# Building one quarter of the scan's transposed input with a diagonal matrix on TensorE, and alternating ScalarE's two kinds of work

## The chip, the cores and the metric

One core of a Trainium2 chip runs the whole program. The metric is the device time of one execution in microseconds (us), as the median of several runs. The engines of the core are called PE (TensorE; PEld are its weight loads), ACT (ScalarE), DVE (VectorE), POOL (GpSimd) and SP (SyncE, which issues DMAs here).

## What is computed

Two layers. Layer 0 is a bidirectional selective state-space block (forward and backward over time) followed by a gated MLP; layer 1 is attention and another MLP. The change touches only the state-space scan. Cut to it:

```python
B, L, D_MODEL, COND = (2, 512, 256, 256)     # the inputs in fact have L = 1024
D_STATE, EXPAND = (64, 2)                     # D_INNER = 512
...
xs = jax.nn.silu(xs)
proj = xs @ xproj_w
dt = jax.nn.softplus(proj[..., :D_INNER] + dt_bias)
Bm = proj[..., D_INNER:D_INNER + D_STATE]
Cm = proj[..., D_INNER + D_STATE:]
A = -jnp.exp(A_log)

def step(hst, ins):
    dt_t, B_t, C_t, x_t = ins
    dA = jnp.exp(dt_t[:, :, None] * A)
    hst = hst * dA + (dt_t * x_t)[:, :, None] * B_t[:, None, :]
    y_t = jnp.einsum('bds,bs->bd', hst, C_t)
    return (hst, y_t)
...
h_fwd = _ssm(h, ...fwd weights...)
h_bwd = jnp.flip(_ssm(jnp.flip(h, 1), ...bwd weights...), 1)
```

For each of the 64 states, the recurrence runs along time for each of 512 channels: the decay is `exp(dt * a)`, the input is `dt * x * B`, and the output sums state times `C` over the states.

## The kernel before, in words

**Units and states.** The scan is cut into 8 units (`UNITS`), each one direction, one batch element and one half (512 steps, `HALF`) of the sequence. A unit has 64 states (`DS`), so the main loop runs over 512 pairs `w = 64 * u + st`. The channels lie in 4 blocks `f` of 128 (`NI`), the 512 time steps in 4 blocks `c` of 128 (`TB`). In half of the units (0, 2, 4 and 6) the scan starts from zero and its last column is saved (`carry`); in units 1, 3, 5 and 7 it starts from that.

**One state, engine by engine.** ACT makes the scan's input with time on the partitions, `uT[t, channel] = dtxT[t, channel] * b[t]`: 4 activations of 128x512 with a scale of one value per partition (line L868), into one of two buffers (`w % 2`). It also makes the decays, 4 exponentials of 128x512 (L875), into one of two buffers. PE turns `uT` over: for each channel block `f`, 4 transposes of 128x128 (`turn_u`, L1421) into one of 3 PSUM banks. DVE runs one scan of 128x512 for each `f` (L1119), reading a decay and a PSUM bank and writing the state's values `hs` (a ring of 3 states). POOL multiplies the values by the row of `C` in two products of 128x1024 (L647), and in units 0, 2, 4 and 6 first copies the last columns to `carry` (L643, with a wait for that copy). PE turns each product back and adds it up over the states in 4 PSUM banks, 16 more transposes for a state (`turn_h`, L1426; for the first state of a unit `first_state` also adds 16 plain f32 products of 128x128, L1446).

**Who waits for whom.** ACT's `uT(w)` waits until PE has turned all of state `w - 2` (`u_full`); its decay `(w, f)` waits for the scan `(w - 2, f)`. `turn_u` waits for all 4 pieces of `uT(w)` and for the scan three tiles back (the bank). A scan waits for its decay, its bank and, in the ring, for the reduction of state `w - 3`. All queues are in order. PE's is `turn_u(w, f)`, then `reduce_state(w - 2, f)`, and after each odd `f` one piece of other work.

**Other work between the states.** The projections of the next unit and the output of the unit before are cut into pieces that PE runs inside the loop (`pe_turn`, `place_turns`): an f32 product of 128x512 at L1213 is a piece, two pieces go into a state, a tile of two products takes one state of two, and a tile of four products (`dt`, `bc`, `out`) two states of three. There are 44 such pieces in a unit (8 for `xs`, 8 for `zs`, 16 for `dt`, 4 for `bc`, 8 for `out`). ACT copies their results (L740, L712, L753, L766) after its 8 activations of a state, and has two bursts in a unit: at state 31 the SiLU of `xs` and `zs` (L745, L747), at state 46 the softplus (L724, L733, L735), both with reloads of its function table. At state 48 POOL has one more product of 128x2048 (L628).

The loop on ACT, and the turn on PE:

```python
if w >= 2:
    act.wait_ge(s["u_full"], NI * (w - 1))
for c in range(TB):
    act.activation(uT[:, w % 2, c], dtxT[:, u % 2, c], ACT.Copy, scale=bT[:, u % 2, c, st:st + 1])\
       .then_inc(s["uT_ready"], 1)
```

Of the kernel before, what the change touches and what calls it, by code (L numbers as in the profile page):

```python
# [11 lines left out]
P = 128  # L12
B, L, DM = 2, 1024, 256
DI, DS = 512, 64
# [4 lines left out]
NI = DI // P  # L19
# [18 lines left out]
SCAN_TILES = UNITS * DS  # L38
# [5 lines left out]
SUMS_STEP = 4  # L44
U_TILES = SCAN_TILES * NI
U_BANKS = 3
RING = 3
PIECES = {"out": 4, "bc": 4, "dt": 4, "down": 4}
SILU_STEP, SOFTPLUS_STEP, DTX_STEP = 31, 46, 48
# [3 lines left out]
def build(nc, t):  # L53
    F32, I32, BF16 = mybir.dt.float32, mybir.dt.int32, mybir.dt.bfloat16
    ALU, ACT, AX = mybir.AluOpType, mybir.ActivationFunctionType, mybir.AxisListType

    ctx = ExitStack()
    with ctx:
        def sb(name, shape, dt=F32):
            return ctx.enter_context(nc.sbuf_tensor(name, shape, dt))  # L60

        def sem(name):
            return ctx.enter_context(nc.semaphore(name))
# [4 lines left out]
        def cut(at, *dims):  # L68
            n = 1
            for d in dims:  # L70
                n *= d
            v = arena[:, at:at + n]
            if len(dims) == 2:
                v = v.rearrange("p (a b) -> p a b", b=dims[1])
            if len(dims) == 3:
                v = v.rearrange("p (a b c) -> p a b c", b=dims[1], c=dims[2])
            if len(dims) == 4:
                v = v.rearrange("p (a b c d) -> p a b c d", b=dims[1], c=dims[2], d=dims[3])
            return v
# [12 lines left out]
        xs = cut(R_XS, 2, NI, HALF)  # L92
        dt_ = cut(R_DT, 2, NI, HALF)
        zsT = cut(R_ZS, 2, HALF // P, DI)

        TB = HALF // P
        dtxT = cut(R_DTX, 2, TB, DI)
        uT = cut(R_UT, 2, TB, DI)  # L100
        decay = cut(R_DA, 2, NI, HALF)
        hs = cut(R_UH, RING, NI, HALF)
        c_rows = cut(R_C, 2, 2, HALF)
# [40 lines left out]
        bT = sb("bT", [P, 2, TB, DS])  # L144
        skip_w = sb("skip_w", [P, 2, NI, P])
        attn_sb = skip_w.rearrange("p a b c -> p a (b c)")
        ident = sb("ident", [P, P])
# [41 lines left out]
        s = {n: sem(n) for n in names}  # L189
# [7 lines left out]
        eaters, first = [], {}  # L197
# [69 lines left out]
        def pe_turn(u, st):  # L267
            return TURN[u].get(st)


        def act_turns(u, st):

            step, long_ = TURN[u].get(st - 1), TURN[u].get(st - 2)
            todo = [long_] if long_ and PIECES.get(long_[0]) else []
            todo += [step] if step and not PIECES.get(step[0]) else []
            if step and step[0] == "sum":
                todo.append(("std",) + step[1:])
            back = TURN[u].get(st - 4)
            if back and back[0] == "mean":
                todo.append(("square",) + back[1:])  # L280
            if u == UNITS - 1:
                return todo
            if st == SILU_STEP:
                todo.append(("silu", u + 1))
            if st == SOFTPLUS_STEP:
                todo.append(("softplus", u + 1))
            return todo
# [90 lines left out]
        place_tiles(START, lambda g: 4 + g % 4)  # L378
        u_before = [holder.get(4 + n) for n in range(U_BANKS)]
        for u in range(UNITS):  # L380
            for st in range(DS):
                if pe_turn(u, st):
                    place_tiles([pe_turn(u, st)], lambda g: 4 + U_BANKS)
        for n in range(U_TILES - U_BANKS, U_TILES):
            holder[4 + n % U_BANKS] = ("u", n)
        place_tiles(LATE, lambda g: 4 + g % 4)
        place_tiles(END, lambda g: 4 + g % 4)

        def eaten(g, who):

            return sum(e == who for e in eaters[:g + 1])
# [20 lines left out]
        def take_u(pe, n):  # L412

            free_bank(pe, u_before[n] if n < U_BANKS else ("u", n - U_BANKS))
            return psum[:, 4 + n % U_BANKS, :]

# [30 lines left out]
        for v in range(BLOCKS):  # L447
            for m in range(BLOCK):
# [4 lines left out]
                if rows_at(v, m):  # L453
                    half, u, j = rows_at(v, m)
# [151 lines left out]
        def _(pool):  # L606
# [23 lines left out]
            for u in range(UNITS):  # L630
                d, b, hi, half = unit(u)
                for st in range(DS):
                    w = u * DS + st
                    p = w // 2
                    h_now = hs[:, w % RING]
                    if w % 2 == 0:
# [38 lines left out]
        def _(act):  # L675
# [99 lines left out]
            def do(order):  # L775

                for kind, *at in order:
                    if kind == "square":
                        square(*at)
                    if kind == "std":  # L780
                        std(*at)
                    if kind in ("xs", "zs"):
                        u, f = at
                        (silu_path if kind == "xs" and u == 0 else raw_path)((xs if kind == "xs" else zsT)[:, u % 2, f], first[kind, u, f])
                    if kind == "silu":
                        silu(*at)
                    if kind == "dt":
                        raw_dt(*at)
                    if kind == "softplus":
                        log_dt(*at)  # L790
                    if kind == "bT":
                        copy_bT(*at)
                    if kind == "dtxT":
                        copy_dtxT(*at)
                    if kind == "yT":
                        copy_yT(*at)
                    if kind == "decay rate":
                        act.wait_ge(s["ssm_small_in"], 80)
                        act.activation(a_neg[:, :, :, :], a_neg[:, :, :, :], ACT.Exp).then_inc(s["a_exp"], 1)
                        skip_weights()  # L800
                    if kind == "up":
                        silu_up(*at)
                    if kind == "qk":
                        copy_qk(*at)
                    if kind == "v":
                        copy_v(*at)
                    if kind == "any key":
                        softmax_scale()
                    if kind == "first part":
                        first_part(*at)  # L810
                    if kind == "second part":
                        act.wait_ge(s["rest_ready"], at[0] + 1)
                        act.activation(qk_parts[:, 1], qk, ACT.Copy).then_inc(s["mid_ready"], 1)
# [42 lines left out]

            do(START)
            act.wait_ge(s["a_ready"], 1)
            for u in range(UNITS):
                d, b, hi, half = unit(u)  # L860
                for st in range(DS):
                    w = u * DS + st
                    if st == 0:
                        act.wait_ge(s["tile_free_act"], eaten(first["dtxT", u, TB - 1], "a"))
                    if w >= 2:
                        act.wait_ge(s["u_full"], NI * (w - 1))
                    for c in range(TB):
                        act.activation(uT[:, w % 2, c], dtxT[:, u % 2, c], ACT.Copy, scale=bT[:, u % 2, c, st:st + 1])\  # L868
                           .then_inc(s["uT_ready"], 1)
                    if st == 0:  # L870
                        act.wait_ge(s["dt_ready"], NI + u)
                    for f in range(NI):
                        if w >= 2:
                            act.wait_ge(s["scan_done"], NI * (w - 2) + f + 1)
                        act.activation(decay[:, w % 2, f], dt_[:, u % 2, f], ACT.Exp, scale=a_neg[:, d, f, st:st + 1])\  # L875
                           .then_inc(s["decay_ready"], 1)
                    do(act_turns(u, st))

            do(LATE)
# [20 lines left out]
            for v in range(BLOCKS):  # L900
                for m in range(BLOCK):
                    w = v * BLOCK + m
# [19 lines left out]
        def _(dve):  # L922
# [183 lines left out]
            for u in range(UNITS):  # L1106
                d, b, hi, half = unit(u)
                for st in range(DS):
# [3 lines left out]
                    for f in range(NI):  # L1112
                        n = NI * w + f
                        if w >= RING:
                            dve.wait_ge(s["reduce_done"], NI * (w - RING) + f + 1)
                        dve.wait_ge(s["decay_ready"], n + 1)
                        dve.wait_ge(s["u_full"], n + 1)
                        way = slice(None, None, -1) if d else slice(None)
                        dve.tensor_tensor_scan(hs[:, w % RING, f, way], decay[:, w % 2, f, way],  # L1119
                                               psum[:, 4 + n % U_BANKS, way],  # L1120
# [88 lines left out]
        def _(pe):  # L1209
# [204 lines left out]
            def turn_u(w, f):  # L1414

                n = NI * w + f
                if f == 0:
                    pe.wait_ge(s["uT_ready"], TB * (w + 1))
                dst = take_u(pe, n)
                for c in range(TB):  # L1420
                    o = pe.transpose(dst[:, c * P:(c + 1) * P], uT[:, w % 2, c, f * P:(f + 1) * P], ident[:, :])  # L1421
                o.then_inc(s["u_full"], 1)

            def turn_h(w, f, c):

                return pe.matmul(psum[:, c, f * P:(f + 1) * P], hs[:, w % RING, f, c * P:(c + 1) * P], ident[:, :],  # L1426
                                 is_transpose=True, start=False, stop=w % DS == DS - 1 and f == NI - 1)
# [28 lines left out]
            for w in range(SCAN_TILES + 2):  # L1456
                u, st = divmod(w, DS)
# [132 lines left out]
```

## Time and profile before

| | |
|---|---|
| median of 3 runs | 3658.23 us (3657.68 to 3658.84) |
| the profiled execution's own time | 3660.08 us |
| its span, from the first to the last instruction | 3658.3 us |
| mean granted TensorE clock | 0.965 |
| the scan (first scan to the end of the last) | 64.8 to 2832.4 us, 76% of the span |
| busy: PE, PEld, DVE, ACT, POOL | 86%, 63%, 82%, 87%, 70% |

The times are read from one profiled execution. PE's busy time is no measure of its capacity, since matmuls overlap; the distance between the starts of two is. The scan takes three quarters of the span, so each engine's share is read inside it, by unit.

### The profile page before, as it was taken

The numbers are of one execution on the slowest core, as the hardware profiler recorded it, in microseconds if no ns is written. First come the engines' busy times: TensorE is split into PE (matmuls) and PEld (weight loads), VectorE is DVE, ScalarE is ACT, GpSimd is POOL, SyncE is SP. The second block draws the span as 40 slices with busy tenths as digits, with TensorE's granted clock in tenths as the row PEclk, the third lists the DMA queues.
The fourth block names the chain that finished last, engine by engine and source line by source line (L and its number), as shares of the span: only waits on it lengthen the run. The fifth ranks groups of instructions, "written<-read, shape, count | busy, mean of one in ns | idle before, by whom it ended". The sixth has DMA issues, their size and how long they took to land.

```text
span 3658.3 us, 55690 instructions
## 1 busy us (share of the span) xinstructions
PE 3164.3 (86%) x20898; PEld 2320.4 (63%) x20898; DVE 3009.3 (82%) x2916; ACT 3179.8 (87%) x5112; POOL 2568.8 (70%) x1577
## 2 busy tenths in 40 slices
PE   8888888889878888988888889878888898999999
PEld 5777777777767777777777777767677432222244
DVE  4888998899889989988998899889999478888241
ACT  6999999999999999999999999999999236777621
POOL 2889998899999979999998899999789000000000
PEclk8999999999999999999999999999999998999999
DMA  2111111111112111111111111112111043121000
GB/s 100 51 44 47 53 53 49 47 53 53 53 42 78 53 48 53 47 54 47 57 54 49 47 53 53 52 44 70 47 47 47 12 104 70 25 29 18 1 6 17
DMA packets 65197, 175.91 MB, mean 48 GB/s; under 512 B 13697, under 2 KB 17537, under 8 KB 64673
## 3 DMA queue, kind: packets, MB, share of 16 engines
q1 hardware_dynamic: 64930, 172.36, 15.3%
q8 instruction: 166, 2.72, 0.3%
q14 instruction: 101, 0.83, 0.1%
HBM read 162.83 MB, written 9.44 MB: 47 GB/s over the span
## 4 chain that ended last, share of the span: by engine, by line
ACT 59%; PE 23%; POOL 11%; DVE 4%; issue 1%; DMA 0%; SPq 0%; DVEq 0%; POOLq 0%; ACTq 0%
ACT arena L868 27%; ACT arena L875 26%; PE psum L1213 10%; POOL arena L647 10%; PE psum L1513 3%; PE psum L1502 3%; PE psum L1477 2%; PE psum L1421 2%; DVE row_max L1166 2%; PE psum L1426 2%; POOL arena L628 1%; DVE arena L1119 1%; PE psum L1446 1%; POOL carry L643 1%; ACT arena L740 1%
## 5 line engine op out<-in xcount | busy, mean ns | idle before, releaser
L647 POOL TENSOR_TENSOR arena<-arena 128x1024 f32<-128x1024 f32 x1024 | 2425.2, 2382 | 172.4 <-DVE arena L1119 128.8
L1421 PE MATMUL psum<-ident,arena 128*128 128x128 f32 x8192 | 1278.7, 280 | 326.0 <-ACT arena L868 268.3
L1421 PEld LDWEIGHTS psum<-ident,arena 128*128 128x128 f32 x8192 | 974.8, 143 | 608.6 <-ACT arena L868 377.0
L868 ACT ACTIVATE arena<-arena,bT 128x512 f32<-128x512 f32 x2048 | 1309.9, 719 | 28.0 <-PE psum L1421 27.8
L1426 PE MATMUL psum<-ident,arena 128*128 128x128 f32 x8192 | 1262.8, 278 | 78.2 <-POOL arena L647 77.3
L1119 DVE TENSOR_TENSOR_SCAN arena<-arena,psum 128x512 f32<-128x512 f32 x1024 | 1179.9, 1204 | 175.2 <-PE psum L1421 94.3
L875 ACT ACTIVATE arena<-arena,a_neg 128x512 f32<-128x512 f32 x2048 | 1311.2, 720 | 1.7 <-DVE arena L1119 1.4
L1119 DVE TENSOR_TENSOR_SCAN arena<-arena,carry,psum 128x512 f32<-128x512 f32 x1024 | 1225.5, 1260 | 96.3 <-ACT arena L875 58.3
L1426 PEld LDWEIGHTS psum<-ident,arena 128*128 128x128 f32 x8192 | 973.5, 143 | 115.5 <-POOL arena L647 115.5
L1213 PE MATMUL psum<-arena 128*128 128x512 f32 x1472 | 709.1, 604 | 12.2 <-issue 5.0
L1213 PEld LDWEIGHTS psum<-arena 128*128 128x128 f32 x1472 | 258.7, 195 | 202.9 <-issue 193.8
L1166 DVE TENSOR_REDUCE row_max<-psum 128x1 f32<-128x512 f32 x512 | 317.9, 676 | 58.1 <-PE psum L1477 56.7
L908 ACT ACTIVATE arena<-psum 128x512 f32<-128x512 f32 x512 | 273.6, 599 | 81.8 <-PE psum L1502 80.1
L670 POOL TENSOR_TENSOR arena<-skip_w 128x512 f32<-128x512 f32 x16 | 20.3, 1267 | 403.6 <-DVE skip_w L1192 403.6
L643 POOL COPY carry<-arena 128x2 f32<-128x2 f32 x512 | 103.9, 203 | 126.4 <-DVE arena L1119 126.0
L1477 PE MATMUL psum<-arena 97*128 97x512 bf16 x512 | 161.3, 393 | 20.1 <-DVE row_max L1166 17.1
L1502 PE MATMUL psum<-arena 100*128 100x512 bf16 x512 | 160.6, 387 | 4.5 <-ACT arena L908 3.4
L663 POOL MEMSET arena<- 4x4096 f32 x3 | 10.7, 3579 | 185.9 <-DVE arena L1041 106.2
L1513 PE MATMUL psum<-arena 128*32 128x512 f32 x1024 | 136.4, 604 | 4.6 <-ACT skip_w L885 4.5
L1502 PEld LDWEIGHTS psum<-arena 100*128 100x128 bf16 x512 | 35.8, 97 | 158.5 <-ACT arena L908 125.0
L825 ACT ACTIVATE arena<-psum,b_up 128x512 f32<-128x512 f32 x32 | 22.0, 687 | 113.4 <-PE psum L1213 113.4
L1477 PEld LDWEIGHTS psum<-arena 97*128 97x128 bf16 x512 | 50.7, 99 | 99.7 <-DVE row_max L1166 45.8
(115 smaller groups left out, 1070.9 us busy)
## 6 DMA issues: line engine op xcount, KB each, us to landing
arena<-bc_dram SPq DMA_DIRECT2D x256, 512.0 KB, 3.7
arena<-qk_dram SPq DMA_DIRECT2D x96, 128.0 KB
qk_dram<-arena SPq DMA_DIRECT2D x12, 512.0 KB, 4.9
arena<-in_x SPq DMA_DIRECT2D x4, 512.0 KB, 10.7
arena<-in_up_w SPq DMA_DIRECT2D x1, 2048.0 KB, 12.0
out_xT<-arena SPq DMA_DIRECT2D x8, 256.0 KB, 2.2
arena<-in_mlp_w SPq DMA_DIRECT2D x3, 512.0 KB, 6.5
arena<-in_fwd_xproj_w SPq DMA_DIRECT2D x1, 1280.0 KB, 9.8
```

Source lines behind the costliest of these rows:

```text
L647: pool.tensor_tensor(h_now[:, f:f + NI // 2], h_now[:, f:f + NI // 2], c_row, ALU.mult)\
L868: act.activation(uT[:, w % 2, c], dtxT[:, u % 2, c], ACT.Copy, scale=bT[:, u % 2, c, st:st + 1])\
L875: act.activation(decay[:, w % 2, f], dt_[:, u % 2, f], ACT.Exp, scale=a_neg[:, d, f, st:st + 1])\
L908: act.activation(probs[:, w % 4, jj], psum[:, n % 3, :], ACT.Exp)\
L1119: dve.tensor_tensor_scan(hs[:, w % RING, f, way], decay[:, w % 2, f, way], psum[:, 4 + n % U_BANKS, way], carry[:, st, f:f + 1] if hi else ...
L1166: dve.tensor_reduce(row_max[:, qt, j, kh:kh + 1], side_bank("scores", w), axis=AX.X, op=ALU.max)\
L1213: o = pe.matmul(dst, lhsT, rhs, start=k == 0, stop=k == len(pairs) - 1)
L1421: o = pe.transpose(dst[:, c * P:(c + 1) * P], uT[:, w % 2, c, f * P:(f + 1) * P], ident[:, :])
L1426: return pe.matmul(psum[:, c, f * P:(f + 1) * P], hs[:, w % RING, f, c * P:(c + 1) * P], ident[:, :], is_transpose=True, start=False, stop ...
L1477: pe.matmul(take_side(pe, "scores", w), stack[u % STACKS][0:PLAIN, 0, j, qt * P:(qt + 1) * P], stack[u % STACKS][0:PLAIN, 1, j, tok(kh)], ...
L1502: pe.matmul(psum[:, n % 3, :], stack[u % STACKS][0:ROWS, 1, j, kt * P:(kt + 1) * P], stack[u % STACKS][0:ROWS, 0, j, tok(qh)], start=True, ...
L1513: o = pe.matmul(psum[32 * j:32 * j + 32, 4, :], v_aug[:, b, kt, hg, 32 * j:32 * j + 32], probs[:, 2 * (kt % 2) + j // 2, j % 2], start=kt ...
```

## The change

Of the 4 time blocks `c` of the scan input, the first (`DIAGS = 1`) is no longer made by ACT over 512 channels. ACT writes only a 128x128 diagonal matrix, the identity times `b[t]`, into `uT[:, w % 2, 0, 0:128]`; PE then multiplies `dtxT` (as weights) by this diagonal, a plain f32 matmul of 128x128, which turns and scales at once. The other three blocks stay transposes.

The order on ACT changes as well: the 4 pieces for `uT(0)` come ahead of the loop, and in state `w` each exponential `f` is followed by piece `f` of `uT(w + 1)`. So `uT` of a state is made one state earlier, and the wait of `uT(w + 1)` for `u_full` stands behind the first exponential of state `w`: it asks for all turns up to state `w - 1`. It is asked for before each piece.

```diff
+DIAGS = 1
...
             do(START)
             act.wait_ge(s["a_ready"], 1)
+            def scan_input(w, c):
+
+                u, st = divmod(w, DS)
+                if st == 0 and c == 0:
+                    act.wait_ge(s["tile_free_act"], eaten(first["dtxT", u, TB - 1], "a"))
+                if w >= 2:
+                    act.wait_ge(s["u_full"], NI * (w - 1))
+                src = ident[:, :] if c < DIAGS else dtxT[:, u % 2, c]
+                act.activation(uT[:, w % 2, c, 0:P if c < DIAGS else DI], src, ACT.Copy,
+                               scale=bT[:, u % 2, c, st:st + 1]).then_inc(s["uT_ready"], 1)
+
+            for c in range(TB):
+                scan_input(0, c)
             for u in range(UNITS):
                 d, b, hi, half = unit(u)
                 for st in range(DS):
                     w = u * DS + st
-                    if st == 0:
-                        act.wait_ge(s["tile_free_act"], eaten(first["dtxT", u, TB - 1], "a"))
-                    if w >= 2:
-                        act.wait_ge(s["u_full"], NI * (w - 1))
-                    for c in range(TB):
-                        act.activation(uT[:, w % 2, c], dtxT[:, u % 2, c], ACT.Copy, scale=bT[:, u % 2, c, st:st + 1])\
-                           .then_inc(s["uT_ready"], 1)
                     if st == 0:
                         act.wait_ge(s["dt_ready"], NI + u)
                     for f in range(NI):
...
                         act.activation(decay[:, w % 2, f], dt_[:, u % 2, f], ACT.Exp, scale=a_neg[:, d, f, st:st + 1])\
                            .then_inc(s["decay_ready"], 1)
+                        if w + 1 < SCAN_TILES:
+                            scan_input(w + 1, f)
                     do(act_turns(u, st))
...
                 for c in range(TB):
-                    o = pe.transpose(dst[:, c * P:(c + 1) * P], uT[:, w % 2, c, f * P:(f + 1) * P], ident[:, :])
+                    if c < DIAGS:
+                        o = pe.matmul(dst[:, c * P:(c + 1) * P], dtxT[:, w // DS % 2, c, f * P:(f + 1) * P],
+                                      uT[:, w % 2, c, 0:P], start=True, stop=True)
+                    else:
+                        o = pe.transpose(dst[:, c * P:(c + 1) * P], uT[:, w % 2, c, f * P:(f + 1) * P], ident[:, :])
                 o.then_inc(s["u_full"], 1)
```

## Rows read from the trace of the kernel before

**Rows 1.** The page: busy time of the engines, and the chain that ended last.

```profile
PE 3164.3 (86%) x20898; PEld 2320.4 (63%) x20898; DVE 3009.3 (82%) x2916; ACT 3179.8 (87%) x5112; POOL 2568.8 (70%) x1577
...
ACT 59%; PE 23%; POOL 11%; DVE 4%; issue 1%; DMA 0%; SPq 0%; DVEq 0%; POOLq 0%; ACTq 0%
ACT arena L868 27%; ACT arena L875 26%; PE psum L1213 10%; POOL arena L647 10%; PE psum L1513 3%; PE psum L1502 3%; PE psum L1477 2%; PE psum L1421 2%; DVE row_max L1166 2%; PE psum L1426 2%; POOL arena L628 1%; DVE arena L1119 1%; PE psum L1446 1%; POOL carry L643 1%; ACT arena L740 1%
```

**Rows 2.** Windows, one for each unit: busy time and count by engine.

```profile
core 0: us, PE busy (x) PEld busy (x) DVE busy (x) ACT busy (x) POOL busy (x), PEclk, DMA share, GB/s
64.80:425.60 360.80, 296.87 (x2172) 254.27 (x2170) 309.43 (x270) 351.41 (x554) 319.62 (x251) 0.95 0.13 46
...
768.40:1112.00 343.60, 291.94 (x2203) 250.63 (x2201) 301.08 (x264) 341.49 (x547) 322.14 (x253) 0.97 0.17 57
1112.00:1454.50 342.50, 291.22 (x2208) 251.60 (x2209) 312.35 (x266) 337.08 (x539) 312.13 (x135) 0.97 0.15 51
...
2484.30:2832.40 348.10, 294.23 (x2196) 254.69 (x2196) 330.95 (x287) 336.81 (x531) 306.43 (x134) 0.96 0.15 48
```

**Rows 3.** Timeline of ACT over one state of unit 2: start, length, instructions.

```profile
1101.36 2.56 ACT L868 ACTIVATE arena<-arena,bT 128x512 f32<-128x512 f32 x4
1103.81 2.56 ACT L875 ACTIVATE arena<-arena,a_neg 128x512 f32<-128x512 f32 x4
1106.27 1.33 ACT L868 ACTIVATE arena<-arena,bT 128x512 f32<-128x512 f32 x2
```

**Rows 4.** Waits in units 1 to 6: us in total, times, longest us.

```profile
ACT arena L868 <- PE psum L1421: 18.3, 12, 4.0
...
POOL arena L647 <- DVE arena L1119: 88.3, 134, 8.6
```

**Rows 5.** Timeline of POOL late in unit 2.

```profile
1086.55 2.38 POOL L647 TENSOR_TENSOR arena<-arena 128x1024 f32<-128x1024 f32 x1
1088.86 0.19 POOL L643 COPY carry<-arena 128x2 f32<-128x2 f32 x1
1089.13 2.38 POOL L647 TENSOR_TENSOR arena<-arena 128x1024 f32<-128x1024 f32 x1
```

**Rows 6.** Timeline of unit 3: DVE, and POOL, each with nothing to wait for.

```profile
1141.68 16.48 DVE L1119 TENSOR_TENSOR_SCAN arena<-arena,carry,psum 128x512 f32<-128x512 f32 x14
...
1398.92 18.68 POOL L647 TENSOR_TENSOR arena<-arena 128x1024 f32<-128x1024 f32 x8
```

**Rows 7.** Timeline of ACT before the scan: the one scaled identity.

```profile
32.51 2.43 ACT L772 ACTIVATE skip_w<-ident,d_skip 128x128 f32<-128x128 f32 x8
```

**Rows 8.** Timeline of PE in unit 1: transposes and plain f32 products of 128x128.

```profile
438.34 2.05 PE L1446 MATMUL psum<-skip_w,arena 128*128 128x128 f32 x8 [0.53 <-POOL arena L647]
...
442.96 0.60 PE L1421 MATMUL psum<-ident,arena 128*128 128x128 f32 x4
443.40 1.06 PE L1446 MATMUL psum<-skip_w,arena 128*128 128x128 f32 x8
444.29 0.60 PE L1426 MATMUL psum<-ident,arena 128*128 128x128 f32 x4
```

**Rows 9.** Timeline of PE in unit 2: a piece, and what follows it.

```profile
1008.03 1.02 PE L1213 MATMUL psum<-arena 128*128 128x512 f32 x2
1008.89 0.60 PE L1421 MATMUL psum<-ident,arena 128*128 128x128 f32 x4
```

**Rows 10.** Groups by line and shape, whole span: busy, mean ns, idle before.

```profile
L628 POOL TENSOR_TENSOR arena<-arena 128x2048 f32<-128x2048 f32 x7 | 31.8, 4541 | 0.0
L875 ACT ACT_TABLE_LOAD x24 | 30.8, 1283 | 0.4
```

**Rows 11.** Timeline of ACT in unit 2, around its burst at state 46.

```profile
1008.05 2.56 ACT L875 ACTIVATE arena<-arena,a_neg 128x512 f32<-128x512 f32 x4
...
1018.21 2.54 ACT L868 ACTIVATE arena<-arena,bT 128x512 f32<-128x512 f32 x4
...
1022.06 2.56 ACT L875 ACTIVATE arena<-arena,a_neg 128x512 f32<-128x512 f32 x4
```

## The prediction

> **What bounds the kernel now.** I read the page first, then the windows by unit, the waits inside the scan, and last the timelines of single states. The page shows three engines above 80% and a chain that runs 53% of its time over two lines of ScalarE, the scan input L868 and the exponentials L875 [rows 1]. The shares are averages over the whole span, so the windows by unit decide [rows 2]: ScalarE is busy 337.1 of 342.5 us in unit 3, 341.5 of 343.6 in unit 2, 351.4 of 360.8 in unit 0, 336.8 of 348.1 in unit 7. Units 1 and 5 are like 3 (342.8 and 342.4), 4 and 6 like 2 (343.7 both). The waits agree: over units 1 to 6 the scan input's copies waited 18.3 us in all, GpSimd's products 88.3 us for scans [rows 4]. So ScalarE's queue, and nothing else, sets the pace almost everywhere.
>
> What stands close behind it matters as much, because it is what is late next. Cadences of a state, each where the engine waits for nothing:
> - ScalarE: its 8 activations start 0.613 us apart, across the switch from copies to exponentials and back as well (1101.36 to 1103.81 to 1106.27) [rows 3]. A state is 4.91 us.
> - GpSimd: in units 0, 2, 4, 6 a product and its carry copy come every 2.58 us, 5.16 us a state [rows 5], already more than ScalarE's 4.91; without the carry 8 products take 18.68 us, 4.67 a state [rows 6]. One 4.5 us product for each later unit comes on top [rows 10].
> - VectorE: 14 scans in 16.48 us, 4.7 us a state, in the units with a carry [rows 6].
> - TensorE: 4 transposes every 0.44 us (0.109 each), so 32 of them 3.49 us; a piece takes 0.86 us (1008.03 to 1008.89) [rows 8, 9].
>
> **The change, part by part.**
>
> *ScalarE's copy shrinks.* 512 copies of 128x512 become 128x128. The nearest row is the same operation on the same identity, scaled by one value per partition: 8 in 2.43 us, 0.30 us each [rows 7]. The saving is 0.613 - 0.30 = 0.31 us a state, 512 x 0.31 = 160 us of ScalarE's work, 20 us a unit. The bounds: 0 if the copy next to exponentials costs as much as a long one, 0.31 + 0.01 at best. I take 0.31, the row being the operation itself. ScalarE's quiet state becomes 4.60 us.
>
> *The order alternates.* Seven switches between copy and exponential a state instead of two. A switch costs nothing in [rows 3], and the exponentials' 24 table loads are three a unit, those after bursts, none between copies and exponentials [rows 10]. I take zero; the bound above is one load of 1.28 us at every switch, which nothing in the rows supports. The extra waits for `u_full` sit on copies that ask again for what the first already had: zero.
>
> *TensorE's matmul.* Per state 4 transposes become 4 plain f32 products of 128x128. They have a row: 8 instructions, which are 4 products, from 443.40 to 444.29, so 0.223 us a product against 0.109 [rows 8]. That is +0.114 each, +0.46 a state; the 16 turns and 16 reductions take 3.95 us. With 44 pieces of 0.86 (38 us), some 9 tiles of 4 transposes and the first state's 16 products (8 us together), a unit is 64 x 3.95 + 46 = 299 us: below every other engine on average. But a state with two pieces is 3.95 + 1.72 = 5.67 us, and in the runs of 4-product tiles (21 states of a unit) the mean is 3.95 + 4 x 0.86 / 3 = 5.10, which is what those states take now by ScalarE: 4.91 and a copy of 0.61 every third state, 5.11. TensorE's own mean there is now 4.64. So there TensorE takes ScalarE's place and the gain is nil.
>
> The Trainium skill (TensorE: Matmul & The Clock Gate, Terms) says that the transpose mode is 4 times faster for f32. Taken as the price of a plain product by size, that would be 0.44 us instead of 0.223, and TensorE's state 4.8 us before any piece; the row of [rows 8] shows twice, and the measured row is what counts. That reading is priced as a rival below.
>
> *The clock.* Where TensorE has just stood still, the same 8 instructions take 2.05 us (438.34) instead of 1.06 [rows 8], at the lower of its two levels; the granted clock of the units is 0.95 to 0.97 [rows 2], although 32 x 64 = 2048 of some 2200 instructions in a unit are transposes. I leave it there. The same page (Part 4: PE-mode transpose) states that transposes do not raise the clock; the 0.97 here says otherwise, and by that rule plain products would bring a gain that I do not count.
>
> *The wait moves.* `uT(w + 1)` asks for the turns of `w - 1` behind the first exponential of `w`, 4.91 - 0.61 = 4.3 us earlier in ScalarE's order than now. Queued behind it are three exponentials, so scans, so GpSimd. The turn it asks for stands in TensorE's queue behind a reduction that waits for GpSimd's product of state `w - 3`. In return, after a burst ScalarE goes to the exponentials at once instead of making 2.45 us of `uT` first: now the first exponential after the softplus burst is 14.0 us behind the one before (1008.05 to 1022.06), 9.1 us over the cadence [rows 11]. I set gain and loss against each other.
>
> **The sum.** By unit, from the spans of [rows 2]:
> - Units 1, 3, 5: ScalarE 337 - 20 = 317 us of work. It waits 5.4 us now, and I add 2 us for the heavier TensorE stretches. About 324 instead of 342.5: 19 us each, 57. The bound: VectorE's 4.7 x 64 plus about 8 us of other work, 309, would make 33 each.
> - Units 2, 4, 6: ScalarE would need 322, but GpSimd cannot go below 64 x 5.16 + 4.5 = 335. Of the 8.8 us above that (bursts, which a ScalarE with slack hides partly, and the unit's border) I let 5 go: 5 each, 15.
> - Unit 0: GpSimd's floor is again 335, ScalarE has many bursts: of 26 us above the floor I take 12.
> - Unit 7: VectorE is busy 331 of 348; of ScalarE's 20 us I take 11.
> - Ahead of and behind the scan: nothing changes.
>
> 57 + 15 + 12 + 11 = 95 us. The profiled execution took 3660.1 us with what lies around its span, so it would take 3565; the median of the runs is 1.9 us lower, which gives 3563 us, 2.6% faster.
>
> **Rivals.**
> - *More is hidden.* The alternate order lets bursts pass without a trace: 33 x 3 + 8.8 x 3 + 26 + 17 = 168 us at the very best, 3490; a half-way case is 3515. For it: GpSimd and VectorE are both under 317 us in units 1, 3, 5. Against: four engines within 3% of each other seldom overlap fully.
> - *TensorE's two-piece states are not levelled out.* There are 22 in a unit, 3 PSUM banks deep. Then a unit is 22 x 5.67 + 42 x 4.7 + 16 us of bursts = 338: 4.5 us less than now, 36 in all, 3622 us (3600 to 3650). Against it: today's two-piece states pass at 5.1 to 5.2 us between lighter ones without a lasting wait.
> - *No difference.* The same with heavy states of 5.9 us, where 22 x 5.9 + 42 x 4.7 + 16 = 343: within 7 us of before.
> - *Slower: the earlier wait closes a loop.* If in every two-piece state ScalarE's first copy waits for the turn behind the reduction, so that TensorE's 5.67 us and one turn more (4 instructions and a product, 0.5 us) come in series, the state is 6.17 us: 22 x 0.27 us over the break-even of 5.9, 6 us a unit, 48 in all, 3706 us. It decides from 5.9 us on. For it: 4.3 us of slack are given away. Against: ScalarE's copies waited 12 times in six units, 18.3 us in all [rows 4].
> - *Slower: plain f32 at four times a transpose.* TensorE's state would be 3.49 + 4 x 0.33 = 4.8 us, the unit 64 x 4.8 + 46 = 353 us: 10 us more than now, 80 in all, 3740 us. Against it stands [rows 8].
>
> **Chances.** Forecast 0.60 (its own range 3530 to 3600), more hidden 0.08, unlevelled TensorE 0.17, no difference 0.06, slower by the loop 0.07, by the price 0.02. The bound of a measurable difference is 0.2%, 7 us. Faster 0.85, same 0.06, slower 0.09. The range reaches down to 3510 and up to 3635 and leaves out the last three cases and the far end of the second.
>
> **What would show it.** Right: the copies of L868's successor in two forms, the short one 0.30 us apart from the next; ScalarE's busy share of units 1, 3, 5 still above 95%, and of units 2, 4, 6 down to about 94% with GpSimd at its 5.16 us; 4096 more short instructions in place of 2048 transposes on TensorE, 0.111 us apart; the units at 324, 338 to 339, 349 and 337 us. Wrong: waits of the copies for TensorE's turns well above 18 us; gaps on ScalarE in states with two pieces; units 1, 3, 5 above 335 us; a table load between copy and exponential. What would make it wrong is a heavy state above 5.7 us, on TensorE's side, or GpSimd's products held back by reductions that come later than now.

## The result and the profile after

The changed kernel took 3631.47 us (3631.32 to 3633.74, 4 runs) against 3658.53 us: a ratio of 0.9924, with a 95% interval of 0.9913 to 0.9936. It is 0.8% faster, where 2.6% were forecast. The time lies in the range that was given, but the gain is 27 us instead of 95.

The page of the changed kernel, busy time by engine and the chain that ended last:

```profile
PE 3354.8 (92%) x22946; PEld 2574.8 (71%) x22946; DVE 3002.5 (83%) x2916; ACT 3032.8 (84%) x5112; POOL 2568.4 (71%) x1577
...
PE 43%; ACT 29%; POOL 20%; DVE 6%; issue 2%; DMA 0%; SPq 0%; DVEq 0%; POOLq 0%; ACTq 0%
POOL arena L649 18%; PE psum L1223 14%; ACT arena L883 12%; ACT arena L869 11%; PE psum L1440 8%; PE psum L1435 6%; PE psum L1432 4%; PE psum L1527 3%; PE psum L1516 3%; PE psum L1491 2%; DVE arena L1129 2%; DVE row_max L1176 2%; POOL carry L645 1%; PE psum L1460 1%; POOL arena L630 1%
```

Against [rows 1] ScalarE lost 147 us of busy time, nearly what was expected, and fell from 59% to 29% of the chain; TensorE went from 23% to 43%. The lines of the changed kernel are L869 (the copies), L883 (the exponentials), L1432 (the plain product), L1435 (transposes of the input), L1440 (transposes of the products), L1223 (the pieces), L1129 (the scans) and L649 (GpSimd).

The groups of ScalarE's two lines and of the plain product, changed kernel (xcount | busy us, mean ns | idle before):

```profile
L883 ACT ACTIVATE arena<-arena,a_neg 128x512 f32<-128x512 f32 x2048 | 1459.3, 713 | 0.3
...
L869 ACT ACTIVATE arena<-arena,bT 128x512 f32<-128x512 f32 x1536 | 1093.8, 712 | 0.0
...
L1432 PE MATMUL psum<-arena 128*128 128x128 f32 x4096 | 831.2, 285 | 133.1 <-DVE arena L1129 91.2 <-ACT arena L869 40.5 <-DVE cmod L951 0.4
...
L869 ACT ACTIVATE arena<-ident,bT 128x128 f32<-128x128 f32 x512 | 203.1, 397 | 153.4 <-PE psum L1435 148.1
```

The short copy is as short as [rows 7] said. But in front of it, and of no other instruction of ScalarE's two lines, stand 148 us of waits for TensorE's turns. It is the first piece of each state, so the one that meets `u_full`.

The windows of units 0 to 3 and 7, changed kernel:

```profile
66.50:421.80 355.30, 322.19 (x2428) 287.78 (x2427) 309.94 (x270) 331.40 (x551) 320.07 (x251) 0.95 0.13 47
421.80:755.50 333.70, 311.50 (x2468) 282.20 (x2469) 310.45 (x266) 320.08 (x543) 309.34 (x134) 0.98 0.15 52
755.50:1097.00 341.50, 312.74 (x2454) 278.99 (x2452) 300.08 (x266) 321.51 (x543) 324.67 (x255) 0.99 0.17 57
1097.00:1433.10 336.10, 315.08 (x2471) 285.34 (x2472) 310.64 (x266) 320.29 (x543) 310.49 (x135) 0.97 0.16 52
2454.70:2804.40 349.70, 322.01 (x2451) 285.96 (x2451) 331.65 (x287) 321.15 (x533) 306.42 (x134) 0.97 0.14 48
```

Beside [rows 2]: unit 0 gained 5.5 us, units 1, 3 and 5 9.1, 6.4 and 6.1, units 2, 4 and 6 2.1, 1.1 and 1.0, and unit 7 lost 1.6. ScalarE is now busy 320 of 336 us in unit 3: it has slack that does not become time.

A unit's window hides where. So this table takes the starts of every fourth scan in the trace and sums the states of a unit by what runs in them (us, means over the units named). "Quiet" states have at most a tile of 4 transposes beside the scan's own work. "Loaded" is the stretch of the `dt` and `bc` tiles.

| states | 0-4 border | 5-10 quiet | 11-18 `out` | 19-30 `xs`, `zs` | 31-32 burst | 33-45 loaded | 46-47 burst | 48-63 | unit |
|---|---|---|---|---|---|---|---|---|---|
| units 1, 3, 5 before | 30.9 | 28.4 | 39.7 | 61.7 | 17.5 | 64.9 | 20.4 | 79.0 | 342.5 |
| changed | 30.9 | 28.2 | 40.7 | 57.7 | 14.7 | 66.8 | 19.0 | 77.4 | 335.3 |
| units 2, 4, 6 before | 28.5 | 28.9 | 39.7 | 61.8 | 16.6 | 65.7 | 20.6 | 81.8 | 343.7 |
| changed | 28.8 | 28.4 | 40.6 | 61.8 | 14.8 | 66.8 | 19.1 | 82.0 | 342.3 |

Three things stand in it. The loaded stretch became slower, 66.8 us in every unit from 0 to 6 (69.4 in unit 7, whose other work is a different one). States 19 to 30 gained 4 us in units 1, 3, 5 and nothing in units 2, 4, 6, where 61.8 us over 12 states are GpSimd's 5.16 a state [rows 5]. And the quiet states had nothing to give in units 1, 3, 5, since 28.4 us over 6 states is 4.7 a state, VectorE's own cadence of [rows 6], already before.

The 4 us of states 19 to 30 end at TensorE, too. Unit 3, changed kernel:

```profile
1197.08:1254.79 57.71, 57.71 (x458) 51.97 (x457) 56.89 (x50) 57.71 (x103) 56.27 (x25) 1.00 0.17 57
```

By the prediction's prices, 12 states of 3.95 us and 12 pieces of 0.86 are 57.7 us.

The loaded stretch of unit 3 in windows, first of the kernel before:

```profile
1290.80:1355.12 64.32, 61.98 (x454) 51.32 (x453) 62.77 (x54) 64.32 (x106) 61.32 (x27) 1.00 0.16 52
```

and of the changed kernel:

```profile
1269.51:1336.31 66.80, 66.80 (x506) 58.20 (x505) 62.92 (x54) 63.31 (x110) 61.77 (x28) 1.00 0.16 50
```

ScalarE was the engine busy for the whole stretch (64.32 of 64.32); now it is TensorE (66.80 of 66.80). One of its two-piece states in the timeline of the changed kernel:

```profile
1329.80 0.38 PE L1432 MATMUL psum<-arena 128*128 128x128 f32 x2
1330.02 0.49 PE L1435 MATMUL psum<-ident,arena 128*128 128x128 f32 x3
1330.35 0.60 PE L1440 MATMUL psum<-ident,arena 128*128 128x128 f32 x4
...
1331.77 1.02 PE L1223 MATMUL psum<-arena 128*128 128x512 f32 x2
1332.63 0.38 PE L1432 MATMUL psum<-arena 128*128 128x128 f32 x2
...
1334.61 1.02 PE L1223 MATMUL psum<-arena 128*128 128x512 f32 x2
1335.47 0.38 PE L1432 MATMUL psum<-arena 128*128 128x128 f32 x2
```

From 1329.80 to 1335.47 is 5.67 us without a gap: 16 turns and 16 reductions, with 4 products of 0.22 us (1329.80 to 1330.02) among them, and two pieces of 0.86. The scans do not all follow at that pace: states 36 to 38 of unit 3, like 39 to 41 and 42 to 44, start 5.67, 4.71 and 4.91 us apart. Together that is 15.29 us for three states, the mean of 5.10 that the prediction gave for TensorE; states 43 to 45 took 15.28 us before, then at ScalarE's pace. What differs is the start of the stretch: before, states 34 to 38 passed at VectorE's 4.69 us, because the scans were still catching up after the burst.

### The profile page after: what moved, and what is told of

Read it like the earlier page. It is cut to its first block, busy times and chain, and to the rows that moved or that the text cites. A ratio compares the mean times of both kernels' runs of the same rounds, so it can differ in the third digit from the quotient of the medians.

```text
span 3629.7 us, 59786 instructions
## 1 busy us (share of the span) xinstructions
PE 3354.8 (92%) x22946; PEld 2574.8 (71%) x22946; DVE 3002.5 (83%) x2916; ACT 3032.8 (84%) x5112; POOL 2568.4 (71%) x1577
## 4 chain that ended last, share of the span: by engine, by line
PE 43%; ACT 29%; POOL 20%; DVE 6%; issue 2%; DMA 0%; SPq 0%; DVEq 0%; POOLq 0%; ACTq 0%
POOL arena L649 18%; PE psum L1223 14%; ACT arena L883 12%; ACT arena L869 11%; PE psum L1440 8%; PE psum L1435 6%; PE psum L1432 4%; PE psum L1527 3%; PE psum L1516 3%; PE psum L1491 2%; DVE arena L1129 2%; DVE row_max L1176 2%; POOL carry L645 1%; PE psum L1460 1%; POOL arena L630 1%
## 5 line engine op out<-in xcount | busy, mean ns | idle before, releaser
L649 POOL TENSOR_TENSOR arena<-arena 128x1024 f32<-128x1024 f32 x1024 | 2425.0, 2384 | 158.8 <-DVE arena L1129 115.9
L883 ACT ACTIVATE arena<-arena,a_neg 128x512 f32<-128x512 f32 x2048 | 1459.3, 713 | 0.3
L1129 DVE TENSOR_TENSOR_SCAN arena<-arena,psum 128x512 f32<-128x512 f32 x1024 | 1175.7, 1204 | 166.2 <-PE psum L1435 101.5
L1440 PE MATMUL psum<-ident,arena 128*128 128x128 f32 x8192 | 1255.0, 277 | 38.4 <-POOL arena L649 38.2
L1129 DVE TENSOR_TENSOR_SCAN arena<-arena,carry,psum 128x512 f32<-128x512 f32 x1024 | 1220.2, 1260 | 83.0 <-ACT arena L883 45.3
L869 ACT ACTIVATE arena<-arena,bT 128x512 f32<-128x512 f32 x1536 | 1093.8, 712 | 0.0
L1435 PE MATMUL psum<-ident,arena 128*128 128x128 f32 x6144 | 1023.5, 276 | 0.0
L1440 PEld LDWEIGHTS psum<-ident,arena 128*128 128x128 f32 x8192 | 969.4, 142 | 67.1 <-POOL arena L649 63.8
L1432 PE MATMUL psum<-arena 128*128 128x128 f32 x4096 | 831.2, 285 | 133.1 <-DVE arena L1129 91.2
L1432 PEld LDWEIGHTS psum<-arena 128*128 128x128 f32 x4096 | 658.0, 194 | 359.1 <-issue 131.7
L1435 PEld LDWEIGHTS psum<-ident,arena 128*128 128x128 f32 x6144 | 756.3, 144 | 0.0
L1223 PE MATMUL psum<-arena 128*128 128x512 f32 x1472 | 708.0, 603 | 27.0 <-ACT arena L749 16.1
L1223 PEld LDWEIGHTS psum<-arena 128*128 128x128 f32 x1472 | 256.9, 194 | 218.9 <-issue 192.9
L869 ACT ACTIVATE arena<-ident,bT 128x128 f32<-128x128 f32 x512 | 203.1, 397 | 153.4 <-PE psum L1435 148.1
L665 POOL MEMSET arena<- 4x4096 f32 x3 | 10.7, 3580 | 185.2 <-DVE arena L1051 105.6
```

The lines of the kernel that those rows point to most:

```text
L649: pool.tensor_tensor(h_now[:, f:f + NI // 2], h_now[:, f:f + NI // 2], c_row, ALU.mult)\
L869: act.activation(uT[:, w % 2, c, 0:P if c < DIAGS else DI], src, ACT.Copy, scale=bT[:, u % 2, c, st:st + 1]).then_inc(s["uT_ready"], 1)
L1223: o = pe.matmul(dst, lhsT, rhs, start=k == 0, stop=k == len(pairs) - 1)
L1432: o = pe.matmul(dst[:, c * P:(c + 1) * P], dtxT[:, w // DS % 2, c, f * P:(f + 1) * P], uT[:, w % 2, c, 0:P], start=True, stop=True)
```

## The experiments

Theory A: TensorE's loaded states take the gain. Theory B: the order does, by its earlier wait for the turns. All ratios are to the kernel before on the same chip; where two kernels are compared in us, it is the difference of their ratios times 3658.5.

**TensorE relieved, all else as changed.** Block 0 is turned by a transpose, which leaves out the factor `b` for that quarter of the scan's input.

```diff
                     if c < DIAGS:
-                        o = pe.matmul(dst[:, c * P:(c + 1) * P], dtxT[:, w // DS % 2, c, f * P:(f + 1) * P],
-                                      uT[:, w % 2, c, 0:P], start=True, stop=True)
+                        o = pe.transpose(dst[:, c * P:(c + 1) * P], dtxT[:, w // DS % 2, c, f * P:(f + 1) * P], ident[:, :])
```

> The changed kernel, but block 0 is turned with a transpose instead of the plain product with the diagonal (it leaves out the factor b for that quarter of the scan's input). ScalarE's work and order are those of the changed kernel, TensorE's load that of the kernel before. Theory A (TensorE's two-piece states at 5.67 us take the gain): those states drop back to 5.2 us, and the time goes to about 3570 us (3550 to 3590). Theory B (the earlier wait for the turns takes it, by GpSimd's and the queue's delay): the waits of the short copy stay near 150 us and the time stays above 3610 us.

Measured: 3580.42 us, 0.9779 (0.9764 to 0.9794), 53 us less than the changed kernel. The loaded stretch of units 1, 3, 5 fell to 61.9 us, 4.8 a state. States 19 to 30 fell from 57.7 to 56.2 us, VectorE's 4.69 a state. The waits of the short copy fell too, to 105 us. Theory A holds for this part. 3580 is not 3570, though: something is left.

**The diagonal alone, in the old order.**

```diff
-            for c in range(TB):
-                scan_input(0, c)
...
                     w = u * DS + st
+                    for c in range(TB):
+                        scan_input(w, c)
...
-                        if w + 1 < SCAN_TILES:
-                            scan_input(w + 1, f)
```

> The diagonal block alone: ScalarE's order is that of the kernel before, four copies, then four exponentials. Theory A: TensorE carries the same load, so 3620 to 3640 us, like the changed kernel. Theory B: the copies no longer wait early, and the time falls under 3605 us.

Measured: 3634.35 us, 0.9930 (0.9915 to 0.9945): as the changed kernel. The loaded stretch is 66.8 us again. By itself this spoke for theory A alone. The table of states says otherwise: state 31 and 32 of units 1, 3, 5 together took 16.1 us here and 14.7 in the changed kernel, while state 31 alone took 9.42 against 9.96. Two effects of opposite sign stood in one number.

**The alternating order alone** (`DIAGS = 0`).

> The alternating order alone (no diagonal, four full copies). Theory A: ScalarE bounds again with the same work; only what the bursts cost changes, 3645 to 3665 us. Theory B: the earlier wait costs by itself, above 3670 us.

Measured: 3672.68 us, 1.0035 (1.0021 to 1.0049). Slower than before, over theory B's bound of 3670 us by little: the order costs by itself, 13 us. That its wait is the reason does not follow from this run (see the run without a diagonal below).

**Copies behind the exponentials.** The four exponentials of a state, then the four copies of the next, then the other work.

```diff
-                        if w + 1 < SCAN_TILES:
-                            scan_input(w + 1, f)
+                    if w + 1 < SCAN_TILES:
+                        for c in range(TB):
+                            scan_input(w + 1, c)
                     do(act_turns(u, st))
```

> The changed kernel with the four exponentials of a state first, then the four copies for the next state, and only then the other work: the wait for the turns comes 1.8 us later in ScalarE's order, and bursts still stand behind the copies. Theory A: no change against the changed kernel, 3625 to 3637 us. Theory B: 3600 to 3615 us, with less than 70 us of waits on the short copy.

Measured: 3593.00 us, 0.9817 (0.9803 to 0.9832), 39 us less than the changed kernel, with the loaded stretch as before at 66.8 us and 105 us of waits on the short copy (not under 70). The gain is larger than theory B's band (3600 to 3615 us), and the sum of waits is a poor measure of it. Most of what changed are the bursts: states 31 and 46 of unit 3 took 8.11 and 10.22 us instead of 9.96 and 12.06, the same 1.84 us in both. Over units 0 to 6 the burst states 31, 32, 46 and 47 gave 26 of the 39 us. The other 13 lie in other states, more than half of them in the first five of a unit and in unit 7, and were not traced to a wait. The run moves the wait and undoes the alternation at once, so it does not yet tell which of the two counts. VectorE's timeline around the burst at state 46 of unit 3, changed kernel:

```profile
1336.31 4.80 DVE L1129 TENSOR_TENSOR_SCAN arena<-arena,carry,psum 128x512 f32<-128x512 f32 x4 [0.38 <-PE psum L1435]
1348.37 2.45 DVE L1129 TENSOR_TENSOR_SCAN arena<-arena,carry,psum 128x512 f32<-128x512 f32 x2 [7.26 <-ACT arena L883]
```

and with the copies behind the exponentials:

```profile
1321.95 4.80 DVE L1130 TENSOR_TENSOR_SCAN arena<-arena,carry,psum 128x512 f32<-128x512 f32 x4 [0.38 <-PE psum L1436]
1332.17 2.45 DVE L1130 TENSOR_TENSOR_SCAN arena<-arena,carry,psum 128x512 f32<-128x512 f32 x2 [5.42 <-ACT arena L883]
```

The scans idle 7.26 us in the one and 5.42 in the other. ScalarE's timeline ahead of the same burst, changed kernel:

```profile
1332.82 0.71 ACT L883 ACTIVATE arena<-arena,a_neg 128x512 f32<-128x512 f32 x1
1334.37 0.40 ACT L869 ACTIVATE arena<-ident,bT 128x128 f32<-128x128 f32 x1 [0.85 <-PE psum L1435]
1334.68 0.71 ACT L883 ACTIVATE arena<-arena,a_neg 128x512 f32<-128x512 f32 x1
...
1338.36 0.66 ACT L714 ACTIVATE arena<-psum,dt_bias 128x512 f32<-128x512 f32 x1
```

and with the copies behind:

```profile
1316.61 2.55 ACT L883 ACTIVATE arena<-arena,a_neg 128x512 f32<-128x512 f32 x4
1320.01 0.40 ACT L869 ACTIVATE arena<-ident,bT 128x128 f32<-128x128 f32 x1 [0.85 <-PE psum L1436]
1320.32 1.93 ACT L869 ACTIVATE arena<-arena,bT 128x512 f32<-128x512 f32 x3
1322.16 0.67 ACT L714 ACTIVATE arena<-psum,dt_bias 128x512 f32<-128x512 f32 x1
```

Both wait 0.85 us for the same turn. From the short copy to the burst's first instruction are 3.99 us in the first and 2.15 in the second. The difference of 1.84 us is three exponentials: they stand between the wait and the burst in the changed kernel, and ahead of the wait in the other.

**The alternating order with a later wait.** A third buffer for the diagonal and block 1 leaves the order and moves the wait alone:

```diff
+        uT_third = sb("uT_third", [P, DI])
+
+        def u_block(w, c):
+            if c > 1:
+                return uT[:, w % 2, c]
+            if c == 0:
+                return uT[:, 0, 0, w % 3 * P:(w % 3 + 1) * P]
+            return uT_third[:, :] if w % 3 == 2 else uT[:, w % 3, 1]
...
-                if w >= 2:
-                    act.wait_ge(s["u_full"], NI * (w - 1))
+                if w >= (2 if c > 1 else 3):
+                    act.wait_ge(s["u_full"], NI * (w - (1 if c > 1 else 2)))
...
```

> The changed kernel, its alternating order kept, but the diagonal and block 1 of the scan's input have a third buffer, so that only the third piece asks for the turns of state w - 1, about 2.1 us later in ScalarE's order. Theory W (what the alternating order loses is the early wait, which cuts ScalarE's lead ahead of a burst): close to the run with the copies behind the exponentials, 3590 to 3602 us, with states 31 and 46 of units 1, 3, 5 about 1.8 us shorter than in the changed kernel. Theory X (decays that come further apart hold the scans up): no change, 3625 to 3637 us.

Measured: 3585.79 us, 0.9796 (0.9779 to 0.9812), 47 us less than the changed kernel and a little below the band. States 31 and 46 of unit 3 took 7.81 and 9.93 us, 2.15 and 2.13 less: the distance by which the wait moved (0.30 + 3 x 0.61). With the diagonal, alternation as such costs nothing; the place of its wait does. In this run, too, the wait is still 109 us long in all.

**The diagonal left out where TensorE is full**, on top of the copies behind.

```diff
+        def diags(w):
+            u, st = divmod(w, DS)
+            long_ = TURN[u].get(st - 1)
+            return 0 if long_ and PIECES.get(long_[0]) else 1
...
-                src = ident[:, :] if c < DIAGS else dtxT[:, u % 2, c]
+                src = ident[:, :] if c < diags(w) else dtxT[:, u % 2, c]
```

> Copies behind the exponentials, and no diagonal in the second state of each tile of four products (7 states of a unit), which stay four transposes and four full copies. TensorE's load there falls by 0.46 us each, ScalarE's rises by 0.31. Theory A (TensorE sets the pace of those stretches): 0.46 x 7 = 3 us less in most units, 3570 to 3585 us, states 33 to 45 of a unit at 65 us instead of 66.8. If ScalarE sets it after all: 3593 us or more.

Measured: 3586.39 us, 0.9798 (0.9783 to 0.9812), about 7 us less than with the copies behind, and 1.4 us over theory A's band. The loaded stretch went to 64.7 us (expected 65), so TensorE sets it; but states 46 and 47 behind it grew from 17.2 to 18.5 us in units 1, 3, 5, which fits that ScalarE with more work has less lead. The interval overlaps that of the run it is compared with.

**Both causes removed.** Copies behind, and block 0 turned by a transpose.

> Both at once: block 0 turned by a transpose (leaves out the factor b for that quarter), copies behind the exponentials. If the two losses add up: 3631 - 51 - 38 = 3542 us. If GpSimd's 5.16 us and VectorE's 4.69 us a state are next: 3555 to 3570 us, with units 2, 4, 6 at 335 to 337 us and units 1, 3, 5 at 322 to 326.

Measured: 3565.16 us, 0.9742 (0.9727 to 0.9757). Not additive: 67 us below the changed kernel, where 53 and 39 would be 92. Like the cheap turn alone, it leaves out the factor `b` for a quarter of the input. Units 2, 4, 6 took 335.1 us, GpSimd's floor of 335 in the prediction; units 1, 3, 5 took 327.5, over the expected 326.

**TensorE's cost alone, on the kernel before.**

```diff
                 for c in range(TB):
-                    o = pe.transpose(dst[:, c * P:(c + 1) * P], uT[:, w % 2, c, f * P:(f + 1) * P], ident[:, :])
+                    if c < 1:
+                        o = pe.matmul(dst[:, c * P:(c + 1) * P], uT[:, w % 2, c, f * P:(f + 1) * P], ident[:, :],
+                                      start=True, stop=True)
+                    else:
+                        o = pe.transpose(dst[:, c * P:(c + 1) * P], uT[:, w % 2, c, f * P:(f + 1) * P], ident[:, :])
```

> The kernel before with nothing but TensorE's cost: block 0 is turned by a plain f32 product with the identity, while ScalarE keeps its four full copies and its order. TensorE's state grows by 0.46 us (plain product 0.223 against 0.109 us, four of them). On average it stays under ScalarE's pace, so if only averages counted the time would be that of before, 3656 to 3664 us; if the two-piece states at 5.67 us count by themselves, 3668 to 3690 us.

Measured: 3676.50 us, 1.0045 (1.0030 to 1.0060): 16 us slower, though ScalarE, and not TensorE, has the larger sum of work in a unit (337 us against 299 by the prediction's count). Its two-piece states took 5.67 us and the loaded stretch 66.8, even with ScalarE's full work.

**Three more.** The third buffer and the copies behind together:

> Copies behind the exponentials and the third buffer for the diagonal and block 1: the wait stands later by both. If ScalarE's lead ahead of a burst is still what is missing: below 3583 us, states 31 and 46 of units 1, 3, 5 below 8.0 and 10.1 us. If TensorE's stretches and the other engines' floors hold now: 3583 to 3592 us.

Measured: 3583.61 us, 0.9792 (0.9778 to 0.9807), the fastest of the kernels that compute everything, though not distinct from the two at 3586. States 31 and 46 of units 1, 3, 5 fell to 7.28 and 9.39 us as the first case had it, but the total did not fall below 3583. Against the third buffer alone the burst states of such a unit gained 1.1 us, and its last 16 states gave 0.9 us back (77.8 against 76.9).

Two blocks by a diagonal (`DIAGS = 2`), copies behind:

> Copies behind the exponentials, and two of the four blocks by a diagonal: ScalarE loses another 0.31 us a state, TensorE gains another 0.46. Theory A (TensorE sets the loaded stretches, 13 states at a mean of 5.14 us): they go to 5.55 us and the two-piece states to 6.13; about 15 us more in units 1, 3, 5, 7 and 11 in the others, 3680 to 3710 us, slower than before. If ScalarE's work still mattered there: under 3600 us.

Measured: 3691.69 us, 1.0088 (1.0073 to 1.0103). The two-piece state is 6.12 us and the loaded stretch 72.6, 5.58 a state and so 0.45 us more for 4 more products. Theory A had said 6.13 and 5.55.

No diagonal, copies behind:

> No diagonal, four exponentials first, then the four full copies of the next state, then the other work: against the kernel before only the place of the other work changes. ScalarE is the bound with the same work, so it has little lead; what it saves is the 2.45 us of copies between a burst and the next exponential: 16 bursts, 3625 to 3655 us.

Measured: 3653.83 us, 0.9984 (0.9974 to 0.9994), 6 us below before: within the band, at its upper end. Against the alternating order alone it is 19 us better. But here the bursts are not the reason: states 31, 32, 46 and 47 of units 1, 3, 5 took 36.9 us with the alternating order and 37.0 with the copies behind. Their quiet states differ, 30.2 against 28.4 us (28.4 before). Unit 3 in these states, alternating order first:

```profile
1146.37:1176.59 30.22, 23.08 (x200) 21.49 (x199) 28.78 (x25) 30.22 (x51) 28.89 (x14) 1.00 0.19 60
```

```profile
1135.74:1164.13 28.39, 24.86 (x200) 21.32 (x199) 28.20 (x26) 28.39 (x48) 28.39 (x14) 1.00 0.19 60
```

ScalarE is busy for all of both (30.22 of 30.22, 28.39 of 28.39), so no wait of it can be what costs the 1.8 us there. A likely reason is that the last exponential of a state stands behind three full copies, 1.84 us later in the queue, so that scans that are catching up run out of decays sooner. No run without the diagonal keeps the alternation and moves the wait alone, so this is not shown.

## Why the prediction was half right

**Right: ScalarE's saving.** The copy of 128x128 takes 0.31 us in the new place (1334.37 to 1334.68), the switches cost nothing, and the table loads of the exponentials are still 24. ScalarE's work in unit 3 fell from 337.1 to 320.3 us by busy time, 17 us where 20 were forecast.

**Right: the prices on TensorE.** A plain product 0.22 us, a two-piece state 5.67, the loaded states at 5.10 on average; 66.8 us over 13 states are 5.14. The Trainium skill's factor of 4 for f32 (TensorE: Matmul & The Clock Gate, Terms) is not what separates a transpose from a plain product here: it is 2 in [rows 8] and in the changed kernel (0.22 us a product, and 3 transposes in 0.33 us, 1330.02 to 1330.35), and the rival built on it (3740 us) is out.

**Wrong: the term of the sum for units 1, 3 and 5**, "ScalarE 337 - 20 = 317 us of work. It waits 5.4 us now, and I add 2 us for the heavier TensorE stretches". The prediction's own part on TensorE had said of these stretches that "the gain is nil"; the sum then counted the saving there all the same. It should have been taken stretch by stretch. By the table, of the 20 us that ScalarE saves in such a unit:
- in states 33 to 45 4 us are saved work and the time rises by 1.9 us, to TensorE's mean; in 11 to 18 it rises by 1.0. Turned cheaply, the same stretches take 61.9 and 39.0 us. The second rival (TensorE's states not levelled out, 3622 us, 3600 to 3650) came nearest in time, but the trace does not show its mechanism: three states take 15.29 us, which is the levelled mean, and not 5.67 + 5.67 + 4.7.
- in states 19 to 30 the time falls by 4.0 us, again to TensorE's mean, and 1.5 us of what VectorE would allow stay.
- in the quiet states, VectorE was at its own 4.7 us already, working off what a burst had left. There ScalarE's saving gives lead and no time.
- in the bursts 4.2 us were gained, and the early wait kept back 1.84 us at each.

So the step that failed is the overlap: TensorE's term was "2 us for the heavier TensorE stretches", and by the run with the cheap turn it is worth 7.2 us in such a unit (335.3 against 328.1).

**Wrong: "I set gain and loss against each other"** for the wait that moved. The gain was real (copies no longer stand behind a burst), and the loss was as large: the changed kernel is level with the diagonal in the old order (3631 and 3634 us), while moving the wait alone gives 47 us. The slower rival had named the wait, but as a loop in the two-piece states; there the state is 5.67 us with either order. With the diagonal it acts mostly through the lead ahead of a burst instead. Without the diagonal the alternating order loses 19 us against the copies behind, and not in the bursts; why is open.

**Mis-sized: the other units.** In units 2, 4, 6 1.4 us came instead of 5; removing either cause alone brings them to 337 us (337.0 with the cheap turn, 337.3 with the copies behind). Unit 0 gave 5.5 instead of 12, unit 7 lost 1.6 instead of gaining 11. Together, 3 x (18.5 - 7.2) + 3 x (5 - 1.4) + 6.5 + 12.6 and a scan that starts 1.7 us later are 66 us, by which the profiled execution (3631.45 us) lies above its forecast of 3565.

With both causes gone the kernel takes 3565 us, 2 us from the forecast. That is partly luck: units 1, 3, 5 took 327.5 us and not 324, units 2, 4, 6 335.1 and not 338.7, unit 0 346.4 and not 349, unit 7 339.3 and not 337. Unit 7, where VectorE's norms come in, was not taken apart: it lost 1.6 us in the changed kernel. The loss goes with the alternating order, which costs it 3.5 us with the diagonal (346.2 us in the old order) and 3.6 without (351.7 against 348.1); by what path stays open.

## What to carry to other kernels

Where four engines lie within a few per cent of each other, sum by stretch and not by period: a saving on the busiest engine is time only in those stretches where it is also the last, and an engine that is 10% below on average can be the bound in those parts of the period where its other work sits. In an in-order queue, look at what stands behind a wait: a wait that is moved ahead of work which doesn't need it can cost that work's length at every burst that follows, and the sum of its waiting time does not show that cost. Such a wait is told from other causes by a buffer more that moves it and nothing else.

## What was not expected of the hardware

Nothing in the prices. The mean granted clock of the profiled execution was 0.970 and 0.971 in the two runs with transposes in place of the plain product, 0.970 and 0.971 in the two with the plain product in the old order, 0.971 in the changed kernel, and 0.975 to 0.979 in the five with plain products and a later wait. TensorE was also busier in those five (93 to 96% of the span, against 89 to 93% in the others), so that the kind of instruction is not shown to be the reason.
